# Decoder layer: in the feed-forward part each unit tile is projected four tiles later, ScalarE squares it twice and GpSimd subtracts

## Chip, cores and metric

The kernel runs on one core of one Trainium2 chip. The metric is device time in microseconds. A core has TensorE (PE in the profile, its weight loads PEld), VectorE (DVE), ScalarE (ACT), GpSimd (POOL) and the queue of SyncE (SP), each with its own instruction stream; they meet by semaphores only.

## What is computed

A decoder layer: linear attention, cross attention and a feed-forward part, each added to its input and normalised over the 256 features of a token. There are 8 batches of 512 tokens. The change touches the feed-forward part alone:

```python
def _L0_ffn_ref(x, fast_b, w_fc, w_proj, u, v, gate):
    ...
    h = _bitlinear(x, w_fc) + gate * (x @ v.T @ fast_b.T @ u.T)
    r = jnp.maximum(h, 0.0)
    return _bitlinear(r * r, w_proj)
...
x = _layernorm(x + _L0_ffn_ref(x, ...), axis=-1)
```

Here `h` has 1024 hidden units, and `_bitlinear` multiplies with a weight matrix that is rounded to three values and scaled.

## The kernel before

Features and hidden units lie on the 128 partitions, tokens in the free dimension. One batch of 512 tokens is 2 tiles of x (256 features) and 8 unit tiles (1024 hidden units), each 128 by 512. Every engine runs its own loop over the 8 batches, written out by hand in `ffn_phase`; the first two and the last two batches stand outside the loop, the four between them in a loop of two batches a turn. The order of the work on an engine is the order in its `batch` function, and nothing moves past a wait.

For precision a float is split in two: a rounded high part and the rest, the low part (`x_hi`, `x_lo`; `h_hi`, `h_lo`). The work on one unit tile i is:

- TensorE, `hidden`: six matmuls into one of the four PSUM banks `HIDDEN` (lines 47 to 49). It waits until ScalarE has read the bank's last content (`relu_out`).
- ScalarE, `hidden`: `r` = Relu of the bank (line 1294), and `h_hi` = Square of `r`, rounded (line 1298).
- GpSimd: `rr` = r * r, not rounded (line 1253).
- VectorE, `hidden_lo`: `h_lo` = `rr` - `h_hi` (line 1378).
- TensorE, `project`: for each of two output halves m, a matmul with `h_hi` and one with `h_lo` (lines 1478, 1479) into the accumulating bank `OUT[:, m]`. Half 0 of all eight tiles is done first, then half 1, after all eight `hidden` of the batch.

`r` and `rr` have four buffers each (RH = 4), so a tile may run four tiles ahead.

Around the unit tiles run two normalisations, of neighbouring batches. In the stretch that PE spends on batch b, the other work is:

- Norm 2 of batch b+1, which makes the input of the next batch: ScalarE squares (`norm2_square`, line 1268), VectorE adds two tiles (line 1334), TensorE `var2` (line 1453, a matmul in full float with a matrix of 1/256), ScalarE `norm2_root` (lines 1277, 1279, 1281), VectorE `normalise2` (lines 1354, 1357, 1365, 1370, 1372). Line 1372 writes `x_lo`, and the first `hidden` of batch b+1 waits for it.
- Norm 3 of batch b-1, the last step of that batch: VectorE `residual` (line 1385, two instructions, reads the banks `OUT`) and `sum_y3` (line 1334), TensorE `mean3` (line 1459), VectorE `deviate3` (line 1392) and `sum_squares3` (lines 1346, 1334), TensorE `var3` (line 1463), ScalarE `norm3_root`, VectorE `normalise3` (lines 1354, 1357, 1398), then the store on SP.

`norm3_root` is the last thing on ScalarE's list for a batch, and `normalise3` the last on VectorE's. The first projection of batch b overwrites `OUT` and waits for `residual(b-1)` (`y3_out`).

Of the kernel before, what the change touches and what calls it, by code (L numbers as in the profile page):

```python
# [16 lines left out]
ACT = mybir.ActivationFunctionType  # L17
ALU = mybir.AluOpType
# [6 lines left out]
P = 128  # L25
B, T, D = 8, 512, 256
DK = D // P
# [7 lines left out]
HK = HID // P  # L35
# [24 lines left out]
def f32(ap):  # L60
    return ap.bitcast(F32)
# [1116 lines left out]
def ffn_phase(nc, ctx, sb, a, c, ps, y2_dram, out):  # L1178
# [5 lines left out]
    tern = sb(ctx, "tern_r", [P, HK, D], F32R)  # L1184
    pscale = c["pscale"]

    def sems(*names):
# [11 lines left out]
    RH = 4  # L1199
    r = sb(ctx, "relu", [P, RH, T], F32)  # L1200
    rr = sb(ctx, "relu2", [P, RH, T], F32)
    h_hi, h_lo = (sb(ctx, "h_" + n, [P, HK, T], F32R) for n in ("hi", "lo"))
# [10 lines left out]
    x_split, h_ps, relu_out, hi_out, rr_out, lo_out, p_ps, y3_out = sems(  # L1213
        "x_split", "h_ps", "relu_out", "hi_out", "rr_out", "lo_out", "p_ps", "y3_out")
# [3 lines left out]
    OUT = ps[:, 5:7, :]  # L1218
# [4 lines left out]
    with nc.Block() as block:  # L1223
# [19 lines left out]
        @block.gpsimd  # L1243
        def _(pool):
            pool.tensor_copy(tern[:], c["tern"][:]).then_inc(tern_out, 1)

            def batch(b, first):
                for i in range(HK):
                    pool.wait_ge(relu_out, HK * b + i + 1)
                    if not (first and i < RH):  # L1250
                        pool.wait_ge(lo_out, HK * b + i - RH + 1)
                    n = i % RH
                    pool.tensor_tensor(rr[:, n, :], r[:, n, :], r[:, n, :], ALU.mult).then_inc(rr_out, 1)  # L1253

            batch(0, True)
            with pool.Fori(1, B) as b:
                batch(b, False)

        @block.scalar
        def _(act):  # L1260
            def norm2_square(b, par):
                if par:
                    act.wait_ge(y_in[1], 8 * (b - 1) + 16)
                elif not (isinstance(b, int) and b == 0):
                    act.wait_ge(y_in[0], 8 * b)
                if not (isinstance(b, int) and b == 0):
                    act.wait_ge(sq2_sum_out, b)
                act.activation(sq2[:], y2[:, par], ACT.Square).then_inc(sq2_out, 1)

            def norm_root(stat, norm, sems, b, first):  # L1270

                est, inv = norm
                var_ps, est_out, rs_out = sems
                act.wait_ge(var_ps, b + 1)
                if not first:
                    act.wait_ge(rs_out, 2 * b)
                act.activation(inv[:], stat, ACT.Ln, bias=c["eps"][:, 0:1]).then_inc(est_out, 1)  # L1277
                act.wait_ge(est_out, 3 * b + 1)
                act.activation(est[:], inv[:], ACT.Exp, scale=-0.5).then_inc(est_out, 1)
                act.wait_ge(est_out, 3 * b + 2)  # L1280
                act.activation(inv[:], est[:], ACT.Square).then_inc(est_out, 1)

            def norm2_root(b, first):
                norm_root(STAT2, (est2, inv2), (var2_ps, est2_out, rs2_out), b, first)

            def norm3_root(b, first):
                norm_root(STAT3, (est3, inv3), (var3_ps, est3_out, rs3_out), b, first)

            def hidden(b, i, first):
                n = HK * b + i  # L1290
                act.wait_ge(h_ps, n + 1)
                if not (first and i < RH):
                    act.wait_ge(rr_out, n - RH + 1)
                act.activation(r[:, i % RH, :], HIDDEN[i % RH], ACT.Relu).then_inc(relu_out, 1)  # L1294
                act.wait_ge(relu_out, n + 1)
                if i == 0 and not first:
                    act.wait_ge(p_ps, 2 * b)
                act.activation(h_hi[:, i, :], r[:, i % RH, :], ACT.Square).then_inc(hi_out, 1)

            def batch(b, par, first, second, last):  # L1300
                for i in (0, 1, 2):
                    hidden(b, i, first)
                if not last:
                    norm2_square(b + 1, 1 - par)
                for i in (3, 4):
                    hidden(b, i, first)
                for i in (5, 6, 7):
                    hidden(b, i, first)
                if not last:
                    norm2_root(b + 1, False)  # L1310
                if not first:
                    norm3_root(b - 1, second)

            act.preload_act_table_set("natural_log_exp_and_others")
            for k in range(DK):
                act.activation(w_hi[:, k], c["wfc"][:, k], ACT.Copy).then_inc(w_round, 1)
            norm2_square(0, 0)
            norm2_root(0, True)
            batch(0, 0, True, False, False)
            batch(1, 1, False, True, False)  # L1320
            with act.Fori(2, B - 3, 2) as i:
                batch(i, 0, False, False, False)
                batch(i + 1, 1, False, False, False)
            batch(B - 2, 0, False, False, False)
            batch(B - 1, 1, False, False, True)
            norm3_root(B - 1, False)

        @block.vector
        def _(dve):
# [41 lines left out]
                dve.wait_ge(x_split, 2 * b + 1)  # L1371
                dve.tensor_tensor(x_lo[:, par], x2[:, par], f32(x_hi[:, par]), ALU.subtract).then_inc(x_split, 1)  # L1372

            def hidden_lo(b, i):
                n = HK * b + i
                dve.wait_ge(hi_out, n + 1)
                dve.wait_ge(rr_out, n + 1)
                dve.tensor_tensor(h_lo[:, i, :], rr[:, i % RH, :], f32(h_hi[:, i, :]), ALU.subtract).then_inc(lo_out, 1)  # L1378

            def residual(b, par, first):  # L1380
                for m in range(DK):
                    dve.wait_ge(p_ps, 2 * b + m + 1)
# [20 lines left out]
            def batch(b, par, first, second, last):  # L1403
                if not first:
                    residual(b - 1, 1 - par, second)
                    sum_y3(b - 1, second)
                hidden_lo(b, 0)
                hidden_lo(b, 1)
                hidden_lo(b, 2)
                if not last:  # L1410
                    sum_squares2(b + 1, False)
                hidden_lo(b, 3)
                if not first:
                    deviate3(b - 1, second)
                for i in (4, 5):
                    hidden_lo(b, i)
                if not first:
                    sum_squares3(b - 1, second)
                for i in (6, 7):
                    hidden_lo(b, i)  # L1420
                if not last:
                    normalise2(b + 1, 1 - par, False)
                if not first:
                    normalise3(b - 1, second)
# [23 lines left out]
        def _(pe):  # L1448
# [16 lines left out]
            def hidden(b, par, i, first):  # L1465
                if i == 0:
                    pe.wait_ge(x_split, 2 * b + 2)
                if not (first and i < RH):
                    pe.wait_ge(relu_out, HK * b + i - RH + 1)
                cols = slice(i * P, (i + 1) * P)  # L1470
                split_matmul(pe, HIDDEN[i % RH], [(w_hi[:, k, cols], w_lo[:, k, cols], x_hi[:, par, k],
                                                   x_lo[:, par, k]) for k in range(DK)]).then_inc(h_ps, 1)

            def project(b, m, tiles):
                for k in tiles:
                    pe.wait_ge(lo_out, HK * b + k + 1)
                    w = tern[:, k, m * P:(m + 1) * P]
                    pe.matmul(OUT[:, m], w, h_hi[:, k, :], start=(k == 0), stop=False)
                    mm = pe.matmul(OUT[:, m], w, h_lo[:, k, :], start=False, stop=(k == HK - 1))
                if tiles[-1] == HK - 1:  # L1480
                    mm.then_inc(p_ps, 1)

            def batch(b, par, first, second, last):
                for i in (0, 1):
                    hidden(b, par, i, first)
                for i in (2, 3):
                    hidden(b, par, i, first)
                if not first:
                    mean3(b - 1, second)
                for i in (4, 5):  # L1490
                    hidden(b, par, i, first)
                if not last:
                    var2(b + 1, False)
                for i in (6, 7):
                    hidden(b, par, i, first)
                if not first:
                    pe.wait_ge(y3_out, 2 * b)
                project(b, 0, range(0, 6))
                if not first:
                    var3(b - 1)  # L1500
                project(b, 0, (6, 7))
                project(b, 1, range(HK))

            var2(0, True)
            pe.wait_ge(w_split, DK)
# [52 lines left out]
```

## Time and profile before

| | us |
|---|---|
| median of 3 runs | 1444.05 |
| lowest and highest | 1442.32, 1445.12 |
| the profiled execution's own time | 1441.72 |
| its span in the profile | 1439.9 |
| PE, DVE, ACT, POOL busy in the span | 1343.1, 956.8, 807.9, 621.9 |
| feed-forward part: first unit matmul to the end of the last instruction | 1238.64 to 1436.76 |

The feed-forward part is the last 198 us of the span. The busy shares of the whole span say little about it; it has to be read in its own window. An instruction's row gives its start, its duration, its engine, its line and, in brackets, for how long the engine had been idle and what ended that. On PE a matmul's record is longer than its share of the engine, since matmuls are pipelined: the distance from one start to the next is the cost.

### The profile page before, as it was taken

What the parts mean: (1) busy time and instruction counts of PE and PEld (TensorE: products, weight loads), DVE (VectorE), ACT (ScalarE), POOL (GpSimd) and SP (SyncE); (2) the same over time, 40 slices, a digit from 0 to 9 for tenths busy, and PEclk for the clock granted to TensorE, in tenths of its full rate; (3) what the DMA queues carried; (4) which work ended last, traced back from release to release, by engine and by line L of the source; (5) the groups of instructions that cost most, each with busy time, mean ns of one, the idle gap of its engine ahead of it and who ended that gap; (6) DMA issues with size and microseconds to landing.
All of it is one profiled execution on the core that took longest, in us unless ns stands there. A gap on an engine that the chain in (4) does not pass through costs nothing. (4 is left out here: it accounts for less than half of the span.)

```text
span 1439.9 us, 20724 instructions
## 1 busy us (share of the span) xinstructions
PE 1343.1 (93%) x7056; PEld 881.1 (61%) x7056; DVE 956.8 (66%) x1806; ACT 807.9 (56%) x1062; POOL 621.9 (43%) x312
## 2 busy tenths in 40 slices
PE   6999768999999999999999999999999997699995
PEld 4777545566566656656665665666566563466663
DVE  6678736765666576566667646666764664599996
ACT  2334435665656566565656656565665654565653
POOL 3513003553545355354535535453553543343432
PEclk9999979999999999999999999999999999799998
DMA  5211220000100100010010001001000100111101
GB/s 175 96 58 47 72 91 1 1 1 1 61 1 1 60 0 0 0 60 0 0 60 0 0 0 60 0 0 60 0 0 0 45 1 15 31 43 44 44 15 44
DMA packets 25535, 42.85 MB, mean 30 GB/s; under 512 B 3441, under 2 KB 7937, under 8 KB 25489
## 3 DMA queue, kind: packets, MB, share of 16 engines
q1 hardware_dynamic: 24672, 39.10, 8.0%
q0 software_dynamic: 816, 3.15, 0.6%
q8 instruction: 27, 0.44, 0.1%
q14 instruction: 20, 0.16, 0.0%
HBM read 29.66 MB, written 12.58 MB: 29 GB/s over the span
## 5 line engine op out<-in xcount | busy, mean ns | idle before, releaser
L907 DVE CUSTOM_DVE_ANT_0 junk<-ps,mask 128x512 bf16<-128x512 f32 x512 | 319.7, 686 | 98.0 <-PE ps L1039 96.8
L729 POOL TENSOR_TENSOR acc<-prob 128x1024 f32<-128x1024 f32 x64 | 153.2, 2394 | 489.1 <-ACT prob L773 489.1
L773 ACT ACTIVATE prob<-ps,mcol 128x1024 f32<-128x1024 f32 x256 | 282.2, 1117 | 135.3 <-PE ps L1033 128.7
L732 POOL TENSOR_TENSOR acc<-acc,prob 128x1024 f32<-128x1024 f32 x128 | 303.9, 2374 | 11.5
L1054 PE MATMUL ps<-prob,v_b 128*64 128x512 f32 x1024 | 244.5, 598 | 0.0
L1054 PEld LDWEIGHTS ps<-prob,v_b 128*64 128x64 f32 x1024 | 67.7, 136 | 133.0 <-issue 109.5
L912 DVE TENSOR_TENSOR ps<-ps,recip 128x512 f32<-128x512 f32 x64 | 44.8, 699 | 155.0 <-ACT recip L788 155.0
L1253 POOL TENSOR_TENSOR relu<-relu 128x512 f32<-128x512 f32 x64 | 79.9, 1252 | 109.1 <-ACT relu L1294 108.9
L1031 PE MATMUL ps<-q_hi,k_hi 64*128 64x512 f32 x512 | 114.7, 443 | 4.1 <-ACT prob L773 1.6
L1039 PE MATMUL ps<-k_hi,q_hi 64*128 64x512 f32 x512 | 103.0, 397 | 4.5 <-DVE nmx L907 2.0
L786 ACT ACTIVATE recip<-ps 128x512 f32<-128x512 f32 x64 | 38.2, 598 | 115.4 <-PE ps L1062 115.4
L1031 PE MATMUL ps<-q_hi,k_lo 64*128 64x512 f32 x512 | 101.6, 392 | 0.0
L1031 PE MATMUL ps<-q_lo,k_hi 64*128 64x512 f32 x512 | 101.6, 391 | 0.0
L1033 PE MATMUL ps<-shift,ones_r 64*128 64x512 f32 x512 | 101.3, 390 | 0.0
L1031 PEld LDWEIGHTS ps<-q_hi,k_hi 64*128 64x128 f32 x512 | 48.3, 184 | 54.7 <-ACT prob L773 24.3
L925 DVE SCALAR_TENSOR_TENSOR att_lo<-ps,bv,att_hi 128x512 fp32r<-128x512 f32 x64 | 48.0, 750 | 49.4 <-ACT att_hi L796 49.4
L1294 ACT ACTIVATE relu<-ps 128x512 f32<-128x512 f32 x64 | 38.2, 597 | 61.3 <-PE ps L49 58.1
L1378 DVE TENSOR_TENSOR h_lo<-relu,h_hi 128x512 fp32r<-128x512 f32 x64 | 62.9, 1021 | 10.7 <-POOL relu L1253 10.7
L796 ACT ACTIVATE att_hi<-ps,bv 128x512 fp32r<-128x512 f32 x64 | 44.1, 689 | 44.9 <-DVE ps L920 44.9
L1062 PE MATMUL ps<-acc,ones_w 128*64 128x512 f32 x256 | 65.8, 592 | 3.3 <-DVE att_lo L925 3.3
L816 ACT ACTIVATE v_b<-ps 128x512 f32<-128x512 f32 x64 | 38.4, 600 | 50.9 <-PE ps L49 50.9
L1045 PEld LDWEIGHTS ps<-ident,nmx 128*128 128x128 f32 x256 | 33.8, 192 | 53.4 <-issue 53.4
(205 smaller groups left out, 2917.0 us busy)
## 6 DMA issues: line engine op xcount, KB each, us to landing
x_in<-in_xT SPq DMA_DIRECT2D x8, 512.0 KB, 3.6
x_scratch<-x_a SPq DMA_DIRECT2D x8, 512.0 KB, 2.8
raw<-x_scratch SPq DMA_DIRECT2D x8, 512.0 KB, 5.1
raw<-in_cT SPq DMA_DIRECT2D x8, 512.0 KB, 6.0
x_res<-x_scratch SPq DMA_DIRECT2D x8, 512.0 KB, 4.5
y_scratch<-y SPq DMA_DIRECT2D x8, 512.0 KB, 3.1
y_c<-y_scratch SPq DMA_DIRECT2D x8, 512.0 KB, 3.6
outT<-x SPq DMA_DIRECT2D x8, 512.0 KB, 2.7
```

The lines of the kernel that those rows point to most:

```text
L729: pool.tensor_tensor(total, prob[:, 0], prob[:, 1], ALU.add).then_inc(acc_out, 1)
L732: pool.tensor_tensor(total, total, prob[:, kt], ALU.add).then_inc(acc_out, 1)
L773: act.activation(prob[:, i].rearrange("p h t -> p (h t)"), SCORE[i % 2].rearrange("p h t -> p (h t)"), ACT.Exp, scale=SCALE, bias=mcol[:, ...
L907: dve.tensor_tensor_reduce(junk[:, t % 2, h], SMAX[t % 2][:, h], mask[:], -1.0, -LOWEST, ALU.add, ALU.min, nmx[:, t, h * DH:h * DH + 1]).t ...
L925: dve.scalar_tensor_tensor(out=att_lo[:, p % HALF], in0=DEN, scalar=c["bv"][:, p:p + 1], in1=f32(att_hi[:, p % HALF]), op0=ALU.add, op1=AL ...
L1031: pe.matmul(banks[:, h], l[OWN[h], par, cols], r[OWN[h], par], start=(n == 0), stop=False)
L1033: mm = pe.matmul(banks[:, h], ones_r[OWN[h], :], shift[OWN[h], :], start=False, stop=True)
L1039: mm = pe.matmul(SMAX[t % 2][:, h], q_hi[OWN[h], par, toks], k_hi[OWN[h], par], start=True, stop=True)
L1054: mm = pe.matmul(PV[OWN[h], :], v[:, kt, cols], prob[:, kt, h, :], start=(kt == 0), stop=(kt == NT - 1))
L1062: mm = pe.matmul(DEN[OWN[h], :], c["ones_w"][:, 0:DH], acc[:, par, h, :], start=True, stop=True)
L1253: pool.tensor_tensor(rr[:, n, :], r[:, n, :], r[:, n, :], ALU.mult).then_inc(rr_out, 1)
L1378: dve.tensor_tensor(h_lo[:, i, :], rr[:, i % RH, :], f32(h_hi[:, i, :]), ALU.subtract).then_inc(lo_out, 1)
```

## The change

The work on a unit tile is dealt out anew, and the projection is woven into the units.

```diff
             def batch(b):
                 for i in range(HK):
-                    pool.wait_ge(relu_out, HK * b + i + 1)
-                    if not (first and i < RH):
-                        pool.wait_ge(lo_out, HK * b + i - RH + 1)
-                    n = i % RH
-                    pool.tensor_tensor(rr[:, n, :], r[:, n, :], r[:, n, :], ALU.mult).then_inc(rr_out, 1)
+                    pool.wait_ge(hi_out, HK * b + i + 1)
+                    pool.wait_ge(rr_out, HK * b + i + 1)
+                    pool.tensor_tensor(h_lo[:, i, :], rr[:, i % RH, :], f32(h_hi[:, i, :]),
+                                       ALU.subtract).then_inc(lo_out, 1)
...
                 act.activation(h_hi[:, i, :], r[:, i % RH, :], ACT.Square).then_inc(hi_out, 1)
+                if not (first and i < RH):
+                    act.wait_ge(lo_out, n - RH + 1)
+                act.activation(rr[:, i % RH, :], r[:, i % RH, :], ACT.Square).then_inc(rr_out, 1)
 
             def batch(b, par, first, second, last):
-                for i in (0, 1, 2):
+                for i in (0, 1):
                     hidden(b, i, first)
                 if not last:
                     norm2_square(b + 1, 1 - par)
-                for i in (3, 4):
-                    hidden(b, i, first)
-                for i in (5, 6, 7):
+                for i in (2, 3, 4, 5):
                     hidden(b, i, first)
                 if not last:
                     norm2_root(b + 1, False)
+                for i in (6, 7):
+                    hidden(b, i, first)
                 if not first:
                     norm3_root(b - 1, second)
...
-            def project(b, m, tiles):
+            def project(b, tiles):
                 for k in tiles:
                     pe.wait_ge(lo_out, HK * b + k + 1)
-                    w = tern[:, k, m * P:(m + 1) * P]
-                    pe.matmul(OUT[:, m], w, h_hi[:, k, :], start=(k == 0), stop=False)
-                    mm = pe.matmul(OUT[:, m], w, h_lo[:, k, :], start=False, stop=(k == HK - 1))
-                if tiles[-1] == HK - 1:
-                    mm.then_inc(p_ps, 1)
+                    for m in range(DK):
+                        w = tern[:, k, m * P:(m + 1) * P]
+                        pe.matmul(OUT[:, m], w, h_hi[:, k, :], start=(k == 0), stop=False)
+                        mm = pe.matmul(OUT[:, m], w, h_lo[:, k, :], start=False, stop=(k == HK - 1))
+                        if k == HK - 1:
+                            mm.then_inc(p_ps, 1)
...
-                for i in (0, 1):
+                for i in (0, 1, 2, 3):
                     hidden(b, par, i, first)
-                for i in (2, 3):
-                    hidden(b, par, i, first)
                 if not first:
                     mean3(b - 1, second)
-                for i in (4, 5):
-                    hidden(b, par, i, first)
+                    pe.wait_ge(y3_out, 2 * b)
+                project(b, (0,))
+                hidden(b, par, 4, first)
+                project(b, (1,))
                 if not last:
                     var2(b + 1, False)
-                for i in (6, 7):
+                for i in (5, 6, 7):
                     hidden(b, par, i, first)
-                if not first:
-                    pe.wait_ge(y3_out, 2 * b)
-                project(b, 0, range(0, 6))
+                    project(b, (i - 3,))
+                project(b, (5, 6))
                 if not first:
                     var3(b - 1)
-                project(b, 0, (6, 7))
-                project(b, 1, range(HK))
+                project(b, (7,))
```

`hidden_lo` and its eight calls a batch are gone from VectorE; what is left there keeps its order. ScalarE's Relu loses its wait on `rr_out`.

Two places of the order matter below. The first is TensorE's list at the end of a batch. Before, `var3` (mean_w times sq_sum, waiting for `c_sq3_sum_out`) stood after six tiles of half 0:

```order
L1478 MATMUL ps<-h_hi,tern_r 128x512 [waits c_lo_out]
L1479 MATMUL ps<-h_lo,tern_r 128x512
L1463 MATMUL ps<-sq_sum,mean_w 128x512 [waits c_sq3_sum_out]
L1476 REGISTER_ALU
L1478 MATMUL ps<-h_hi,tern_r 128x512 [waits c_lo_out]
L1479 MATMUL ps<-h_lo,tern_r 128x512
```

After it came ten tiles of projection (20 matmuls) and then the next batch. In the changed kernel it stands behind tile 6, with the four matmuls of tile 7 between it and the next batch's first unit:

```order
L1464 MATMUL ps<-h_hi,tern_r 128x512 [waits c_lo_out]
L1465 MATMUL ps<-h_lo,tern_r 128x512
L1464 MATMUL ps<-h_hi,tern_r 128x512
L1465 MATMUL ps<-h_lo,tern_r 128x512
L1448 MATMUL ps<-sq_sum,mean_w 128x512 [waits c_sq3_sum_out]
L1461 REGISTER_ALU
L1464 MATMUL ps<-h_hi,tern_r 128x512 [waits c_lo_out]
L1465 MATMUL ps<-h_lo,tern_r 128x512
L1464 MATMUL ps<-h_hi,tern_r 128x512
L1465 MATMUL ps<-h_lo,tern_r 128x512
L1452 REGISTER_ALU
L1454 ISA [waits c_x_split]
```

So 16 of the 20 matmuls that stood between `var3` and the next batch are now ahead of `var3`.

The second place is ScalarE's list around `norm2_root` of the next batch (the three rows of `est2`). Before, it came after tile 7, and `norm3_root` (`var3_ps`) followed at once:

```order
L1294 ACTIVATE relu<-ps 128x512 [waits c_rr_out,c_h_ps]
L1298 ACTIVATE h_hi<-relu 128x512 [waits c_relu_out]
L1274 REGISTER_ALU
L1276 REGISTER_ALU [waits c_var2_ps]
L1277 ACTIVATE inv<-ps,eps 128x512 [waits c_rs2_out]
L1278 ISA
L1279 ACTIVATE est<-inv 128x512 [waits c_est2_out]
L1280 REGISTER_ALU
L1281 ACTIVATE inv<-est 128x512 [waits c_est2_out]
L1276 ISA [waits c_var3_ps]
```

Now two whole unit tiles, of three instructions each, stand behind it:

```order
L1275 ACTIVATE inv<-ps,eps 128x512 [waits c_rs2_out]
L1276 ISA
L1277 ACTIVATE est<-inv 128x512 [waits c_est2_out]
L1278 REGISTER_ALU
L1279 ACTIVATE inv<-est 128x512 [waits c_est2_out]
L1289 REGISTER_ALU
L1290 ACTIVATE relu<-ps 128x512 [waits c_h_ps]
L1294 ACTIVATE h_hi<-relu 128x512 [waits c_relu_out]
L1297 ACTIVATE relu<-relu 128x512 [waits c_lo_out]
```

The root for the next batch moved ahead of the last two tiles, and line 1297 is the second Square (the rows call both `r` and `rr` "relu").

## Rows read from the trace of the kernel before

**Rows 1.** Windows: length, busy PE, PEld, DVE, ACT, POOL, clock, DMA, GB/s.

```profile
1330.00:1354.00 24.00, 21.90 (x87) 15.96 (x88) 23.44 (x24) 14.48 (x23) 9.80 (x8) 1.00 0.14 45
1427.00:1440.00 13.00, 2.08 (x2) 0.50 (x2) 5.42 (x6) 1.95 (x3) 0.00 (x0) 0.50 0.11 40
```

**Rows 2.** Groups by line in the feed-forward part, VectorE's subtraction.

```profile
L1378 DVE TENSOR_TENSOR h_lo<-relu,h_hi 128x512 fp32r<-128x512 f32 x64 | 62.9, 1021 | 10.7 <-POOL relu L1253 10.7
```

**Rows 3.** Timeline: the first unit matmul of batches 0, 2, 4 and 7.

```profile
1238.64 0.76 PE L47 MATMUL ps<-cx_hi,wfc_hi 128*128 128x512 f32 x1 [6.95 <-DVE cx_lo L1372]
1282.57 0.49 PE L47 MATMUL ps<-cx_hi,wfc_hi 128*128 128x512 f32 x1 [0.21 <-DVE cx_lo L1372]
1330.08 0.49 PE L47 MATMUL ps<-cx_hi,wfc_hi 128*128 128x512 f32 x1 [0.40 <-DVE cx_lo L1372]
1401.08 0.50 PE L47 MATMUL ps<-cx_hi,wfc_hi 128*128 128x512 f32 x1
```

**Rows 4.** Timeline of batch 4: GpSimd and VectorE at the same time.

```profile
1332.60 1.40 DVE L1385 SCALAR_TENSOR_TENSOR y<-ps,pscale,x 128x512 f32<-128x512 f32 x2
1333.98 1.04 POOL L1253 TENSOR_TENSOR relu<-relu 128x512 f32<-128x512 f32 x1 [0.33 <-ACT relu L1294]
1334.04 1.52 DVE L1334 TENSOR_TENSOR y_sum<-y 128x512 f32<-128x512 f32 x1
...
1344.21 2.06 DVE L1346 TENSOR_TENSOR sq<-dev 128x1024 f32<-128x1024 f32 x1
1345.24 1.93 POOL L1253 TENSOR_TENSOR relu<-relu 128x512 f32<-128x512 f32 x1
```

**Rows 5.** Timeline of batch 4 on TensorE, the last unit matmul before mean3, and behind it.

```profile
1335.44 0.39 PE L49 MATMUL ps<-cx_hi,wfc_lo 128*128 128x512 f32 x1
1335.70 1.12 PE L1459 MATMUL ps<-y_sum,mean_w 128*128 128x512 f32 x2
1336.89 0.39 PE L48 MATMUL ps<-cx_lo,wfc_hi 128*128 128x512 f32 x1
```

**Rows 6.** GpSimd's subtraction early in the kernel (line 241); VectorE's cast (timeline).

```profile
L241 POOL TENSOR_TENSOR wq_lo<-raw,wq_hi x4: 1265/1272/2135, 23.7 to 30.9; 128x512 fp32r<-128x512 f32 x4
53.52 1.67 DVE L426 CAST og_hi<-sq_a 128x1024 fp32r<-128x1024 f32 x1
```

**Rows 7.** Timeline of ScalarE: two roots' ends, and three unit instructions in a row.

```profile
1231.73 0.69 ACT L1277 ACTIVATE inv<-ps,eps 128x512 f32<-128x512 f32 x1 [2.89 <-PE ps L1453]
1233.11 0.63 ACT L1281 ACTIVATE inv<-est 128x512 f32<-128x512 f32 x1
...
1248.14 0.58 ACT L1294 ACTIVATE relu<-ps 128x512 f32<-128x512 f32 x1
1248.75 0.63 ACT L1298 ACTIVATE h_hi<-relu 128x512 fp32r<-128x512 f32 x1
1249.29 0.58 ACT L1294 ACTIVATE relu<-ps 128x512 f32<-128x512 f32 x1
```

**Rows 8.** Timeline of VectorE: the steps of the normalisation.

```profile
1233.77 0.75 DVE L1354 SCALAR_TENSOR_TENSOR rs<-ps,eps,inv 128x512 f32<-128x512 f32 x1 [3.07 <-ACT inv L1281]
1325.82 0.69 DVE L1357 SCALAR_TENSOR_TENSOR rs<-rs,est 128x512 f32<-128x512 f32 x1
1326.64 1.22 DVE L1365 SCALAR_TENSOR_TENSOR x<-y_c,rs 128x1024 f32<-128x1024 f32 x1
1327.99 0.69 DVE L1370 CAST cx_hi<-x 128x1024 fp32r<-128x1024 f32 x1
1328.72 1.23 DVE L1372 TENSOR_TENSOR cx_lo<-x,cx_hi 128x1024 fp32r<-128x1024 f32 x1
```

**Rows 9.** Timeline of the tail: last projection, mean3, var3.

```profile
1422.70 0.39 PE L1479 MATMUL ps<-h_lo,tern_r 128*128 128x512 f32 x1
1425.45 1.12 PE L1459 MATMUL ps<-y_sum,mean_w 128*128 128x512 f32 x2 [2.36 <-DVE y_sum L1334]
1429.88 2.08 PE L1463 MATMUL ps<-sq_sum,mean_w 128*128 128x512 f32 x2 [3.30 <-DVE sq_sum L1334]
```

More of the change, by code:

```diff
@@ L1245, in _, with batch @@
             pool.tensor_copy(tern[:], c["tern"][:]).then_inc(tern_out, 1)
-            def batch(b, first):
+            def batch(b):
                 for i in range(HK):
-                    pool.wait_ge(relu_out, HK * b + i + 1)
-                    if not (first and i < RH):
-                        pool.wait_ge(lo_out, HK * b + i - RH + 1)
-                    n = i % RH
-                    pool.tensor_tensor(rr[:, n, :], r[:, n, :], r[:, n, :], ALU.mult).then_inc(rr_out, 1)
-            batch(0, True)
-            with pool.Fori(1, B) as b:
-                batch(b, False)
+                    pool.wait_ge(hi_out, HK * b + i + 1)
+                    pool.wait_ge(rr_out, HK * b + i + 1)
+                    pool.tensor_tensor(h_lo[:, i, :], rr[:, i % RH, :], f32(h_hi[:, i, :]),
+                                       ALU.subtract).then_inc(lo_out, 1)
+            with pool.Fori(0, B) as b:
+                batch(b)
         @block.scalar
@@ L1291, in hidden @@
                 act.wait_ge(h_ps, n + 1)
-                if not (first and i < RH):
-                    act.wait_ge(rr_out, n - RH + 1)
                 act.activation(r[:, i % RH, :], HIDDEN[i % RH], ACT.Relu).then_inc(relu_out, 1)
@@ L1372, in normalise2 @@
                 dve.tensor_tensor(x_lo[:, par], x2[:, par], f32(x_hi[:, par]), ALU.subtract).then_inc(x_split, 1)
[L1374 to L1378, printed above, removed]
             def residual(b, par, first):
@@ L1406, in batch @@
                     sum_y3(b - 1, second)
-                hidden_lo(b, 0)
-                hidden_lo(b, 1)
-                hidden_lo(b, 2)
                 if not last:
                     sum_squares2(b + 1, False)
-                hidden_lo(b, 3)
                 if not first:
                     deviate3(b - 1, second)
-                for i in (4, 5):
-                    hidden_lo(b, i)
                 if not first:
                     sum_squares3(b - 1, second)
-                for i in (6, 7):
-                    hidden_lo(b, i)
                 if not last:
@@ L1489, in batch @@
                     mean3(b - 1, second)
-                for i in (4, 5):
-                    hidden(b, par, i, first)
+                    pe.wait_ge(y3_out, 2 * b)
+                project(b, (0,))
+                hidden(b, par, 4, first)
+                project(b, (1,))
                 if not last:
                     var2(b + 1, False)
-                for i in (6, 7):
+                for i in (5, 6, 7):
                     hidden(b, par, i, first)
-                if not first:
-                    pe.wait_ge(y3_out, 2 * b)
-                project(b, 0, range(0, 6))
+                    project(b, (i - 3,))
+                project(b, (5, 6))
                 if not first:
                     var3(b - 1)
-                project(b, 0, (6, 7))
-                project(b, 1, range(HK))
+                project(b, (7,))
             var2(0, True)
```

## The prediction

> **What bounds the kernel now.** I read the feed-forward part alone, by three views. The timeline gives the first unit matmul of each batch [rows 3]: batches 0 and 1 take 43.93 us together (21.97 each), batches 2 to 6 take 118.50 (23.70 each), and from batch 7's first matmul to the end, at 1436.76, it is 35.68. The sum is 198.1. The windows show who is full [rows 1]: in 24 us of a steady batch VectorE is busy 23.44, TensorE 21.90 (its records overlap), ScalarE 14.48, GpSimd 9.80. So VectorE sets the batch. The groups say with what [rows 2]: 64 subtractions, 62.9 us, 7.9 us a batch, 1021 ns each.
>
> Why 1021 ns, for an instruction that takes 0.68 alone? Rows 4 show it. GpSimd works from 1333.98 to 1335.02. VectorE's y_sum, begun at 1334.04, ends at 1335.56, 0.54 after GpSimd. The square of 1024 columns ends at 1346.27, and GpSimd's product, begun under it at 1345.24, ends 0.90 behind that. So these two never run together: the later one ends a full duration less 0.15 after the earlier. The two residual instructions, which read PSUM, run beside a product of GpSimd at their usual 0.7. I call instructions with two SBUF inputs on VectorE "exclusive"; the cast behaves like one too (1.67 at 53.52 against 0.69 alone) [rows 6, 8].
>
> The Trainium skill agrees, in "GPSIMD Engine Reference", Key points: GpSimd shares its SBUF interfaces with VectorE and contends with instructions of two SBUF inputs or in a two-port mode.
>
> **Unit costs.** TensorE, start to start: from 1330.08 to 1335.44 are 23 matmuls, 0.1 of it start-up, so 0.229 each [rows 3, 5]. A unit tile is 6 x 0.229 = 1.37, a projected tile 4 x 0.229 = 0.91. A full-float matmul: from 1335.44 to 1336.89 with two ordinary ones in it, 1.45 - 0.46 = 0.98 [rows 5]. TensorE's own work in a batch is 8 x 1.37 + 8 x 0.91 + 3 x 0.98 = 21.2.
>
> ScalarE: Relu to Square is 0.61, Square to an independent instruction 0.54 [rows 7]. The second Square is not in the trace; its nearest row is the first, 0.63. So a tile is now 0.61 + 0.54 + 0.54 = 1.7, against 1.15, and a root is 1231.73 to 1233.74, 2.0 [rows 7]. ScalarE's sum, 8 x 1.7 + 2 x 2.0 + 1.0 = 18.6, fits beside 21.2.
>
> GpSimd: the subtraction from two tiles to a rounded one is line 241: 1.27 at its least [rows 6], against 1.04 for r * r [rows 4]. Bounds: 1.04 below, 2.13 above (the stretched maximum there). I take 1.27, since shapes and types are the same. Eight are 10.2 us; with VectorE's exclusive ones (about 9.0) that is 19.2, under 21.2.
>
> The Trainium skill, in "GPSIMD Engine Reference", Engine selection, speaks against the move: elementwise work with two inputs is about 2 times slower on GpSimd than on VectorE. By it the subtraction would be some 1.35 (twice 0.68) instead of 1.27, an estimate, and the sum below about 1.3 us higher. That GpSimd is the slower one agrees with the rows (1.27 against 0.68).
>
> So by busy time alone the batch would fall from 23.7 to about 21.2. The question is whether the waits allow it.
>
> **The ring.** I lay one batch out with these costs; 0 is its first unit matmul.
>
> 1. The norm 3 root of the batch before ends at 1.37 on ScalarE (its place follows from step 6). VectorE then needs 0.77 + 0.82 + 1.16 for the three steps of normalise3, 1.4 for the two residuals [rows 4, 8], and is at y_sum at 5.6. There GpSimd has just begun tile 1 (5.40 to 6.67), so y_sum ends at 6.67 + 0.54 = 7.2.
> 2. TensorE has done tiles 0 to 3 at 5.5 and stands at mean3 until 7.34: a wait of 1.85. Behind it in the queue are all the rest.
> 3. mean3 0.98, projection of tile 0 0.91, unit 4 1.37, projection 1 0.91, var2 0.98, unit 5 1.37: 13.85. ScalarE starts tile 5 at 14.13, is through at 15.84, and the root for the next batch ends at 17.85.
> 4. VectorE: two steps (0.77, 0.82), then x from 19.47 to 20.70, exclusive [rows 8]. ScalarE meanwhile does tile 6 and hands it over at 19.71. GpSimd has to wait for x: 20.70 + 1.27 - 0.15 = 21.82.
> 5. TensorE, ready for tile 6 since 20.2, gets it at 21.93: a wait of 1.7. Then 0.91 and 0.1 start-up, var3 at 22.94, 0.98, and tile 7 at 23.91 (its subtraction is done at 23.5, behind the cast). 0.91 more: the next batch starts at 24.82. x_lo, held up by both, ends at 24.56, just in time.
> 6. var3's result is there at 24.06, the root runs from 24.18 to 26.19, which is 1.37 in the next batch. The ring is closed.
>
> **A steady batch is 24.8 us, 1.1 more than before.** What carried it: before, 20 matmuls stood behind var3 and hid the root and normalise3 (about 4.6 us of cover). Now there are four; so the chain root, normalise3, residual, y_sum, mean3 lies bare, and in the same lap TensorE waits for x, which comes late because mean3 came late. The 7.9 us that VectorE loses are not on this ring, apart from the h_lo instructions that it no longer meets.
>
> **The sum.** Batch 0 has no norm 3 and starts at the low clock as before; the same laying-out gives 23.4 (21.92 before), since its end has the collision of step 4 too. Batch 1, with mean3 in time, gives 23.1 (22.01 before). Batches 2 to 6: 5 x 24.82 = 124.1, against 118.5. Batch 7: TensorE ends at 22.0, but norm 3 of batch 6 runs only behind var3, so y_sum is done at 28.3 and mean3 starts at 28.45, against 24.37 in the rows (1425.45 - 1401.08) [rows 3, 9]. From there it is the same chain. That is 4.1 more. TensorE has then stood idle for over 6 us; in the rows it ran var3 at half clock after a pause of 3.3, in 2.08 instead of 1.12 [rows 1, 9], so mean3 costs 0.96 more as well.
>
> 1.5 + 1.1 + 5.6 + 4.1 + 0.96 gives 13.3. Before's own time of 1441.7 becomes 1455.0. The median of the runs shown is 2.3 above that execution; on its scale it is 1457.3. I say 1457.
>
> **Rivals.**
>
> - *The exclusion does not bite (12 in 100).* If the new subtraction ran beside VectorE, steps 1, 4 and 5 lose their stretches: y_sum ends at 6.3, tile 6 is there at 21.0 at once. The same laying-out then gives 23.05 a batch. 198.1 becomes about 199.5: time 1445, no difference that can be told. Against it: rows 4, where every meeting shows it; for it: the rows are of a product of one tile with itself.
> - *GpSimd comes first at tile 6 (8 in 100).* In step 4 x is 0.24 ahead. If GpSimd wins, tile 6 is 1.1 earlier and the lap is about 24.0: time 1452.
> - *TensorE becomes the bound: faster (8 in 100).* If the chain behind var3 and the one behind var2 were both covered, the batch would be TensorE's 21.2: 7 x (21.2 - 23.2) is 14 less, the tail's 4 to 5 come on top, time 1434. It decides from the point where the lap without stretches, 23.05, is 1.8 shorter than I lay out; no row is that far off.
> - *The subtraction is slow, near 2.1 (4 in 100).* GpSimd and VectorE together then exceed 25 a batch: 7 x 2 us more, time above 1465. For it: only the one stretched row [rows 6].
> - The ring as laid out: 68 in 100, with a range of its own of 1451 to 1462 (subtraction 1.04: 3 less; 1.5: 4 more).
>
> **The numbers.** Predicted 1457. From 1445 (no exclusion) to 1463 about 8 in 10 are covered. A measurement tells 0.2%, some 3 us, from no change: slower 0.80, same 0.12, faster 0.08.
>
> **What the profile of the changed kernel should show.** VectorE's busy time in a steady 24 us falls from 23.4 to about 15 to 16, ScalarE's rises to about 19; neither is full. Starts of batches 24.8 apart. TensorE idle before mean3 (line 1444), waiting for y_sum, about 1.8 us, and before line 1464 at tile 6, waiting for h_lo, about 1.7, in each of batches 2 to 6. GpSimd's subtraction alone 1.27, stretched to 2.1 at tile 6; VectorE's cast and x_lo stretched to 1.5 and 2.2. mean3 of the last batch 28 us after its first matmul and at half clock. I am wrong if the waits at mean3 are missing, or if the batches stand under 23.5 apart.

## The result

| | before | changed |
|---|---|---|
| median, us | 1444.31 (1442.32 to 1445.12, 4 runs) | 1453.09 (1451.56 to 1457.09, 4 runs) |
| ratio to before | | 1.007 (95% interval 1.0057 to 1.0084) |
| own time of the profiled execution | 1441.72 | 1457.09 |
| feed-forward part in the trace | 198.1 | 208.7 |

The changed kernel is 0.7% slower. Its profiled execution entered the feed-forward part 4.7 us later than that of before (1243.37 against 1238.64 [rows 3]), though nothing ahead of it was changed, so the two own times should not be compared. The granted clock was at half for 59.5 us ahead of that point, against 47.3 us in the execution of before; whether that is all of the 4.7 is not shown. The feed-forward parts can be compared, and differ by 10.6 us. The interval of the ratio is 8 to 12 us.

The page of the changed kernel, with each engine's busy time in the whole span:

```profile
PE 1347.8 (93%) x7056; PEld 885.8 (61%) x7056; DVE 907.4 (62%) x1742; ACT 837.8 (58%) x1126; POOL 636.9 (44%) x312
```

And the window of one steady batch, 24 us long, columns as in [rows 1]:

```profile
1338.96:1362.96 24.00, 21.02 (x85) 15.73 (x85) 16.54 (x15) 17.63 (x31) 11.90 (x8) 1.00 0.13 44
```

VectorE fell from 23.44 to 16.54, ScalarE rose to 17.63, GpSimd to 11.90. No engine is full any more (TensorE is busy for 21.02 of the 24 us), and yet the batch is longer. Something waits. The view of waits in the feed-forward part says for what (engine, line, releaser, us in total, times, longest; other waits left out at the dots):

```profile
...
DVE rs L1353 <- ACT inv L1279: 63.8, 16, 11.3
...
ACT inv L1275 <- PE ps L1448: 30.9, 8, 12.4
PEld ps L1464 <- POOL h_lo L1251: 16.7, 15, 1.8
PE ps L1444 <- DVE y_sum L1333: 15.1, 7, 6.0
...
PE ps L1464 <- POOL h_lo L1251: 10.0, 8, 1.4
...
DVE dev L1385 <- PE ps L1444: 6.6, 7, 2.2
```

TensorE now waits at mean3 (line 1444) for y_sum and at a projection (line 1464) for GpSimd's subtraction; VectorE waits for both roots, and ScalarE for var3 (line 1448). The timeline of TensorE over the end of batch 4, 1338.96 being that batch's start, shows both waits and the next start:

```profile
1346.27 1.12 PE L1444 MATMUL ps<-y_sum,mean_w 128*128 128x512 f32 x2 [1.59 <-DVE y_sum L1333]
...
1360.59 0.50 PE L1464 MATMUL ps<-h_hi,tern_r 128*128 128x512 f32 x1 [1.39 <-POOL h_lo L1251]
...
1361.64 1.02 PE L1448 MATMUL ps<-sq_sum,mean_w 128*128 128x512 f32 x2
...
1363.44 0.49 PE L47 MATMUL ps<-cx_hi,wfc_hi 128*128 128x512 f32 x1
```

The bracket counts from the modelled end of the last matmul. By starts, less the 0.229 us of one matmul, TensorE stood idle 1.75 us before mean3 (1344.29 to 1346.27) and 1.55 us before the projection of tile 6 (1358.81 to 1360.59). The batch took 24.48 us. The chain of the work that ended last, in that stretch, goes round once (start, us, what; "issue" is time with no wait that the profile shows):

```profile
1339.58 0.64 ACT inv L1279
1340.25 0.76 DVE rs L1353
1341.03 0.70 DVE rs L1356
...
1342.99 1.42 DVE y L1378 x2
1344.43 1.72 DVE y_sum L1333
...
1346.27 1.12 PE ps L1444 x2
...
1352.87 0.61 ACT relu L1290
...
1358.37 2.17 POOL h_lo L1251
1360.59 0.50 PE ps L1464
...
1361.80 0.87 PE ps L1448 x2
1362.78 0.70 ACT inv L1275
```

It leaves ScalarE's root of norm 3, passes VectorE, mean3, unit tile 5, ScalarE's root of norm 2 and its work on tile 6, GpSimd's subtraction of tile 6 and var3, and is back at the same root, whose first step began at 1338.19 in the lap before and begins at 1362.78 in this one, 24.6 us later.

The instructions stretched by the exclusion, on VectorE and on GpSimd in the same batch (alone they take 0.69, 1.23 and 1.29):

```profile
1359.54 1.54 DVE L1369 CAST cx_hi<-x 128x1024 fp32r<-128x1024 f32 x1
1361.12 2.19 DVE L1371 TENSOR_TENSOR cx_lo<-x,cx_hi 128x1024 fp32r<-128x1024 f32 x1
1358.37 2.17 POOL L1251 TENSOR_TENSOR h_lo<-relu,h_hi 128x512 fp32r<-128x512 f32 x1 [2.28 <-ACT relu L1297]
1360.50 1.73 POOL L1251 TENSOR_TENSOR h_lo<-relu,h_hi 128x512 fp32r<-128x512 f32 x1
```

And the tail, where mean3 of the last batch, after a pause of 6 us, ran at the lower of the clock's two levels (granted clock 0.50 from 1439.85 to 1441.95; 2.07 us instead of 1.12 in [rows 9]):

```profile
1439.85 2.07 PE L1444 MATMUL ps<-y_sum,mean_w 128*128 128x512 f32 x2 [5.99 <-DVE y_sum L1333]
```

### The profile page after: what moved, and what is told of

It is laid out like the page before. It is cut to its first block and busy times, and to the rows that moved or that the text cites. A ratio compares the mean times of both kernels' runs of the same rounds, so it can differ in the third digit from the quotient of the medians.

```text
span 1455.3 us, 20590 instructions
## 1 busy us (share of the span) xinstructions
PE 1347.8 (93%) x7056; PEld 885.8 (61%) x7056; DVE 907.4 (62%) x1742; ACT 837.8 (58%) x1126; POOL 636.9 (44%) x312
## 5 line engine op out<-in xcount | busy, mean ns | idle before, releaser
L1251 POOL TENSOR_TENSOR h_lo<-relu,h_hi 128x512 fp32r<-128x512 f32 x64 | 94.4, 1482 | 107.0 <-ACT relu L1297 106.9
L47 PE MATMUL ps<-bc_hi,wk_hi 128*128 128x512 f32 x128 | 54.0, 422 | 11.7 <-DVE bc_lo L881 11.7
L1464 PE MATMUL ps<-h_hi,tern_r 128*128 128x512 f32 x128 | 55.1, 431 | 10.0 <-POOL h_lo L1251 10.0
```

What stands on the lines that cost most here:

```text
L47: pe.matmul(out, lh, rh, start=(i == 0), stop=False)
L1251: pool.tensor_tensor(h_lo[:, i, :], rr[:, i % RH, :], f32(h_hi[:, i, :]), ALU.subtract).then_inc(lo_out, 1)
```

## The experiments

All eight were timed in rounds with the kernel before on the same chip; its median there was 1443.17 beside e1 to e4 and 1442.54 beside e5 to e8. For each the table gives the median, the ratio to before, and from its trace a steady batch (mean of batches 2 to 6), the tail (batch 7's first matmul to the end) and the whole feed-forward part, in us. For the two kernels of the study, a steady batch is 23.70 and 24.39, the tail 35.7 and 40.1, the part 198.1 and 208.7.

| run | median | ratio (95%) | batch | tail | part |
|---|---|---|---|---|---|
| e1 changed, var3 early | 1440.14 | 0.9978 (0.9967 to 0.999) | 22.74 | 35.7 | 195.6 |
| e2 division of work alone | 1440.97 | 0.9986 (0.9975 to 0.9998) | 23.04 | 33.9 | 197.0 |
| e3 order alone | 1463.69 | 1.0144 (1.0127 to 1.0161) | 24.93 | 40.1 | 217.7 |
| e4 changed, rs in PSUM | 1446.82 | 1.0027 (1.0017 to 1.0037) | 23.53 | 40.1 | 201.9 |
| e5 e1, root of norm 2 early | 1433.28 | 0.9936 (0.992 to 0.9953) | 21.69 | 35.7 | 188.9 |
| e6 e5, square of norm 2 first | 1428.02 | 0.9898 (0.9882 to 0.9915) | 20.88 | 36.4 | 184.1 |
| e7 e6, rs in PSUM | 1429.42 | 0.991 (0.989 to 0.9929) | 20.87 | 36.5 | 183.4 |
| e8 before, var3 late | 1450.78 | 1.0057 (1.004 to 1.0073) | 23.97 | 42.3 | 206.7 |

### e1: var3 early

```diff
-                for i in (5, 6, 7):
+                for i in (5, 6):
                     hidden(b, par, i, first)
                     project(b, (i - 3,))
-                project(b, (5, 6))
+                hidden(b, par, 7, first)
                 if not first:
                     var3(b - 1)
-                project(b, (7,))
+                project(b, (4, 5, 6, 7))
```

> Changed kernel with one edit: on TensorE the variance matmul of norm 3 (var3) stands right behind unit tile 7 instead of behind the projection of tile 6, so 16 matmuls of projection and not 4 lie between it and the next batch. Theory (the ring through var3, root, normalise3, residual, y_sum, mean3): the wait at mean3, 1.5 us in each steady batch of the changed kernel's trace, is gone, and with it the delay that it passes on; a steady batch falls from 24.4 to about 23.0 us, the last batch's tail from 40.1 to about 36.5, the feed-forward part from 208.7 to about 198, the time to about 1442. Rival (the exclusion of GpSimd and VectorE at tile 6 sets the batch, and would set it anyway): the wait at mean3 goes but comes back at tile 6; the batch stays within 0.3 of 24.4, and only the tail gains 3 us: about 1449.

Measured: 1440.14, batch 22.74, tail 35.7. The theory's numbers hold (1442, about 23.0, about 36.5 were expected), and the rival (24.4 within 0.3) falls. The waits of TensorE in that run's steady batch, by its timeline:

```profile
1337.12 1.12 PE L1444 MATMUL ps<-y_sum,mean_w 128*128 128x512 f32 x2
...
1348.07 1.02 PE L1448 MATMUL ps<-sq_sum,mean_w 128*128 128x512 f32 x2
1351.45 0.50 PE L1464 MATMUL ps<-h_hi,tern_r 128*128 128x512 f32 x1 [0.52 <-POOL h_lo L1251]
1353.14 0.50 PE L1464 MATMUL ps<-h_hi,tern_r 128*128 128x512 f32 x1 [0.48 <-POOL h_lo L1251]
```

mean3 starts without a bracket: it waits for nobody. One matmul, moved ahead of twelve projection matmuls (2.7 us), takes all of the loss back and a little more. What is left are two short waits for the subtractions of tiles 6 and 7.

### e2: the division of work alone

The changed kernel with TensorE's `project` and `batch` and ScalarE's `batch` of the kernel before; ScalarE squares twice and GpSimd subtracts.

> One part of the change alone: ScalarE squares twice and GpSimd subtracts, but TensorE and ScalarE keep the order of the kernel before (half 0 of all tiles, then half 1, var3 with ten tiles of projection behind it, both roots behind tile 7). Theory (order, not the division of work, costs the time): var3's chain is covered again; about 23.4 us a steady batch, tail as in the kernel before or 1 us shorter, time 1440 to 1445. Rival (the slower subtraction on GpSimd, 1.29 against 0.68, costs the time): 24.4 us a batch as in the changed kernel, about 1450 or more.

Measured: 1440.97, batch 23.04. The theory holds and the rival falls: with the old order the slower subtraction does not make the kernel slower (it leaves one short wait, 0.43 in the second row below), and taking eight subtractions from VectorE gains 0.7 us a batch. That is little beside the 7.9 us of VectorE's time that they were, because the batch now ends at another wait:

```profile
1335.84 0.49 PE L47 MATMUL ps<-cx_hi,wfc_hi 128*128 128x512 f32 x1 [1.12 <-DVE cx_lo L1371]
1353.49 0.50 PE L1463 MATMUL ps<-h_hi,tern_r 128*128 128x512 f32 x1 [0.43 <-POOL h_lo L1251]
1358.98 0.49 PE L47 MATMUL ps<-cx_hi,wfc_hi 128*128 128x512 f32 x1 [1.12 <-DVE cx_lo L1371]
```

The two batches shown begin 1.12 us late for x_lo: ScalarE starts the root of norm 2 at 1351.92, directly behind tile 7's second Square (1351.40 to 1352.01), and VectorE's x_lo ends at 1358.86.

### e3: the order alone

The kernel before with the changed TensorE and ScalarE orders; GpSimd multiplies and VectorE subtracts.

> The other part alone: TensorE's and ScalarE's new order, but GpSimd multiplies and VectorE subtracts as in the kernel before. Theory: the chain behind var3 lies bare here too, with VectorE's eight subtractions on top of it; laid out from the rows of the kernel before it is 24.8 us a steady batch, tail 38 to 39: about 1455 to 1460. Rival (the division of work costs it, the order is harmless): 23.7 us a batch as before, 1444.

Measured: 1463.69, batch 24.93, tail 40.1, batches 0 and 1 25.8 and 27.2. The harm is in the order, and is larger with the old division of work: 20.5 us against the 8.8 of both parts together. The rival (1444) falls. The batch of 24.93 is close to the 24.8 that I expected, but the mechanism that I gave for it is not what the trace shows: in the steady batches TensorE does not wait at mean3 at all (its one wait there, 6.0 us, is in the tail). It waits at the start of every next batch for x_lo. The waits of the whole part, and then of four batches (1316 to 1416):

```profile
PE ps L1459 <- DVE y_sum L1334: 6.0, 1, 6.0
```

```profile
PE ps L47 <- DVE cx_lo L1372: 10.0, 4, 2.5
```

The end of batch 3 shows where x_lo is held up:

```profile
1334.24 2.04 DVE L1378 TENSOR_TENSOR h_lo<-relu,h_hi 128x512 fp32r<-128x512 f32 x2 [1.00 <-POOL relu L1253]
1336.21 0.74 DVE L1354 SCALAR_TENSOR_TENSOR rs<-ps,eps,inv 128x512 f32<-128x512 f32 x1
...
1339.89 1.23 DVE L1372 TENSOR_TENSOR cx_lo<-x,cx_hi 128x1024 fp32r<-128x1024 f32 x1
1341.25 0.49 PE L47 MATMUL ps<-cx_hi,wfc_hi 128*128 128x512 f32 x1 [2.53 <-DVE cx_lo L1372]
```

Here `normalise2` stands behind `hidden_lo` of tile 7 on VectorE's list, and the woven order brings tile 7 later (its Relu begins 16.9 us into the batch). In the changed kernel VectorE has no `hidden_lo`, so this wait is not in it, and this run does not test the ring of the changed kernel; e1 does. That the forecast of the batch came out was luck.

The time lies 4 us above the range that I gave, and the two batches that stick out are 1 and 4, with 27.2 and 26.1. In both the granted clock was at half for a stretch (columns as in [rows 1]):

```profile
1263.90:1270.70 6.80, 6.13 (x14) 4.79 (x15) 3.32 (x5) 1.82 (x3) 1.04 (x1) 0.50 0.20 70
1342.40:1345.80 3.40, 3.40 (x10) 2.62 (x9) 3.24 (x5) 1.23 (x2) 1.04 (x1) 0.50 0.30 112
```

At half clock a matmul takes 0.43 us from start to start instead of 0.229. Batch 4 is 1.4 us longer than its neighbours. For batch 1 about 3 us is an estimate, from half of the 6.1 us of it at half clock. So part of the 20.5 us is the clock's, which the changed kernel lost only at its start and in its tail.

### e4: the reciprocal roots in PSUM

```diff
-                inverse_root((STAT2, est2, inv2, rs2), est2_out, rs2_out, b)
+                inverse_root((STAT2, est2, inv2, STAT2), est2_out, rs2_out, b)
...
-                dve.scalar_tensor_tensor(out=x2[:, par], in0=y2[:, par], scalar=-0.5, in1=both(rs2), op0=ALU.mult,
+                dve.scalar_tensor_tensor(out=x2[:, par], in0=y2[:, par], scalar=-0.5, in1=both(STAT2), op0=ALU.mult,
```

The same for norm 3; `var2` and `mean3` then wait for `x2_out` and `x3_out` instead of `rs2_out` and `rs3_out`.

> Changed kernel, but the reciprocal roots rs of both norms are written in place into their PSUM banks, so that the second step of each root and the products x and x3 have one SBUF input and one PSUM input and should run beside GpSimd. Theory (exclusion): GpSimd's subtraction of tile 6 takes 1.29 and not 2.17, TensorE's wait at tile 6 falls by 0.9, a steady batch from 24.4 to about 23.6, the first two by 0.9 each; the wait at mean3 stays near 1.5: feed-forward part 208.7 to about 203, time about 1447. Rival (the stretch comes from something else, such as the two instructions' memory traffic in general): tile 6's subtraction stays above 2 us and the time at 1453.

Measured: 1446.82, batch 23.53, part 201.9: as the theory said. Its timeline of VectorE and GpSimd at tile 6:

```profile
1352.38 1.22 DVE L1364 SCALAR_TENSOR_TENSOR x<-y_c,ps 128x1024 f32<-128x1024 f32 x1
1352.54 1.29 POOL L1251 TENSOR_TENSOR h_lo<-relu,h_hi 128x512 fp32r<-128x512 f32 x1 [2.28 <-ACT relu L1297]
1353.73 0.69 DVE L1369 CAST cx_hi<-x 128x1024 fp32r<-128x1024 f32 x1
```

x (1352.38 to 1353.60) and the subtraction (1352.54 to 1353.83) overlap by 1.06 us and neither is stretched; in the changed kernel the same pair gave 1.23 and 2.17. What the edit changed in this pair is that one of x's inputs comes from PSUM. The step that now writes rs into PSUM takes what it took before, 0.70 against 0.69 us. What the edit takes of the exclusion was worth 6.3 us by the medians (1453.09 to 1446.82) and 6.8 by the traces (208.7 to 201.9).

### e5: the root of norm 2 early, on top of e1

```diff
-                for i in (2, 3, 4, 5):
+                for i in (2, 3):
                     hidden(b, i, first)
                 if not last:
                     norm2_root(b + 1, False)
-                for i in (6, 7):
+                for i in (4, 5, 6, 7):
                     hidden(b, i, first)
...
                 project(b, (0,))
+                if not last:
+                    var2(b + 1, False)
                 hidden(b, par, 4, first)
                 project(b, (1,))
-                if not last:
-                    var2(b + 1, False)
```

> On top of the early var3: the root of norm 2 for the next batch stands two unit tiles earlier on ScalarE (behind tile 3, not 5) and its variance matmul right behind the projection of tile 0. Theory (with mean3 on time, the next thing that ends last in a batch is normalise2 colliding with the subtractions of tiles 6 and 7): moved away from them, a steady batch falls from 22.8 us to about 21.8, batch 0 by 0.5: feed-forward part about 189, time 1433. Rival (TensorE's own work, 21.2 by its rows, plus small gaps is already the bound at 22.8): no change, 1440.

Measured: 1433.28, batch 21.69, part 188.9: the theory to the microsecond; the rival falls.

### e6: the square of norm 2 first, on top of e5

```diff
-                for i in (0, 1):
-                    hidden(b, i, first)
                 if not last:
                     norm2_square(b + 1, 1 - par)
-                for i in (2, 3):
+                for i in (0, 1, 2, 3):
                     hidden(b, i, first)
```

> On top of that, the square for norm 2 stands first in ScalarE's batch instead of behind tile 1, where it can run while TensorE makes the first unit tile. Theory: the variance matmul no longer comes late, normalise2 is through before tile 6, and the batch is TensorE's own work, about 21.1 to 21.4 us; feed-forward part 184 to 186, time about 1429. Rival (ScalarE is the bound by then): 21.8 as in the run before it.

Measured: 1428.02, 1.0% under the kernel before; the part of 184.1 is as expected, and the batch of 20.88 lies a little under the 21.1 to 21.4 that I gave. The rival (21.8) falls. The window of a steady stretch, columns as in [rows 1]:

```profile
1339.00:1363.00 24.00, 24.00 (x99) 18.31 (x98) 21.07 (x18) 20.73 (x37) 15.51 (x10) 1.00 0.13 44
```

TensorE is busy for all of the 24 us and at full clock: the feed-forward part is bound by TensorE's own work, 20.88 a batch. This version beats both kernels, and no other is measurably faster.

### e7: rs in PSUM, on top of e6

> The kernel of the run before with rs of both norms kept in PSUM. Theory: once TensorE is the bound, the exclusion of GpSimd and VectorE costs nothing, so the 6.3 us that this edit gave the changed kernel are no longer there: within 1 us of the run before. Rival (the stretches still delay TensorE): 3 to 6 us less than the run before.

Measured: 1429.42, that is 1.4 us above e6 where I expected at most 1; single runs lie between 1426.9 and 1432.29, and the intervals of e6 and e7 overlap. The rival (3 to 6 us less) falls. The steady batch is the same (20.87); only batch 0 is 0.7 us shorter. The edit that was worth 6.3 us in the changed kernel is worth nothing measurable here. In e6 instructions are still stretched (in this batch x 2.12, the cast 1.58, a subtraction 2.03), but TensorE, busy all the time in the window above, does not wait for any of them:

```profile
1336.91 2.12 DVE L1362 SCALAR_TENSOR_TENSOR x<-y_c,rs 128x1024 f32<-128x1024 f32 x1
1339.16 1.58 DVE L1367 CAST cx_hi<-x 128x1024 fp32r<-128x1024 f32 x1
1338.15 2.03 POOL L1251 TENSOR_TENSOR h_lo<-relu,h_hi 128x512 fp32r<-128x512 f32 x1 [0.21 <-ACT relu L1297]
```

### e8: the kernel before with var3 late

```diff
-                project(b, 0, range(0, 6))
+                project(b, 0, range(HK))
+                project(b, 1, range(0, 6))
                 if not first:
                     var3(b - 1)
-                project(b, 0, (6, 7))
-                project(b, 1, range(HK))
+                project(b, 1, (6, 7))
```

> The kernel before with one edit: var3 stands in front of the last four projection matmuls (tiles 6 and 7 of half 1) instead of in front of the last twenty. Theory (what hides the root and normalise3 is the projection behind var3, whoever subtracts): a steady batch rises from 23.7 to 24.2 or more, and the tail from 35.7 by 4 to 6 us with its mean3 at half clock: feed-forward part 198 to about 207, time 1450 to 1455. Rival (the place of var3 matters only with the new division of work): 1443 in the batches, at most 4 us in the tail.

Measured: 1450.78, 8.2 us more than before for one moved matmul, of about the size of the whole change. The time is in the range, but not put together as I expected: the tail took most of it (42.3 against 35.7, 6.6 us where I gave 4 to 6), and a steady batch rose by 0.27 alone, less than 0.5. In the steady batches the result is thus nearer to the rival than to the theory, though the wait at mean3 is there:

```profile
1338.59 1.12 PE L1459 MATMUL ps<-y_sum,mean_w 128*128 128x512 f32 x2 [1.72 <-DVE y_sum L1334]
```

In the kernel before, VectorE's work was the limit (busy for 23.23 of the 23.78 us of batch 3), and TensorE had slack beside it. By starts, TensorE stood idle there for 1.3 us at var2, 0.7 at var3 and 0.6 for x_lo, 2.6 together; in e8 it is 1.9 at mean3 and 0.9 for a subtraction, 2.7 together. The new wait took the place of the old ones.

## Why the prediction was right

The forecast was 1457 in a range of 1445 to 1463, slower with 0.8; measured were 1453.09. The likeliest case was the one that came.

- **The ring (steps 1 to 6).** Right for the changed kernel, and shown by e1: with var3 moved and nothing else, the wait at mean3 is gone, and the batch falls from 24.39 to 22.74. The laps' pieces, as laid out and as in the trace of batch 4: root's end to mean3's start 5.97 and 6.06; mean3 to tile 5's Relu 6.79 and 6.60; that to x's start 5.34 and 5.32; x to the projection of tile 6 2.46 and 2.40; that to the next start 2.89 and 2.85; start to root's end 1.37 and 1.25. The sum is 24.82 and 24.48. The largest miss is the full-float matmul, sized 0.98 from a row that held some start-up of TensorE as well. Between running neighbours it takes 0.86, from the start of var2 to the second matmul behind it, 1.09, less one ordinary matmul, 0.229:

```profile
1350.43 1.02 PE L1438 MATMUL ps<-sq_sum,mean_w 128*128 128x512 f32 x2
1350.89 0.79 PE L47 MATMUL ps<-cx_hi,wfc_hi 128*128 128x512 f32 x1
1351.52 0.39 PE L48 MATMUL ps<-cx_lo,wfc_hi 128*128 128x512 f32 x1
```

  With it TensorE's own work is 20.8 a batch and not 21.2, which fits the 20.88 of e6.
- **The exclusion.** Right: tile 6's subtraction 2.17 (2.1 forecast), the cast 1.54, x_lo 2.19 (1.5 and 2.2). e4 shows the cause, and the price of the part that it takes away.
- **The subtraction's price.** 1.29 alone, against 1.27 from [rows 6]; so the rival of a subtraction near 2.1 fell. e2 shows that this price was not what cost the time. The Trainium skill's factor of 2 over VectorE ("GPSIMD Engine Reference", Engine selection) fits as well (1.29 over 0.68 is 1.9).
- **The rival of GpSimd first at tile 6** did not come: x began first in all seven batches, in batch 4 by 0.18 us (1358.19 against 1358.37; 0.24 forecast). That is a narrow margin.
- **The rival of no exclusion** was at 1445; the measured time lies beyond it, and e4 shows that the exclusion is real. Its 23.05 a batch was not tested: e4 takes away the part of x and x3 and has a batch of 23.53, with y_sum still stretched (1.56 to 1.74 us in the steady batches, against 0.69 alone) and mean3 still waiting.
- **The rival of TensorE as the bound** was right on what stands in the way (the chains behind var3 and var2) and it is what e5 and e6 reach by covering both.
- **The sum, 13.3**, was too large. Against the 10.6 of the traces: batches 2 to 6 gave 3.5 and not 5.6, that is 0.4 a batch less; batch 1 gave 0.6 and not 1.1; the tail 4.4 and not 5.1; and batch 0 gave 2.2 and not 1.5, since TensorE ran at half clock for its first 5.4 us and not 3.9 as in the kernel before, and half of that difference, an estimate of what the clock cost, is the missing 0.7. The term that was mis-sized is the steady batch, for the reason above. The clock's 0.7 has nothing to do with the change and hid part of that miss by chance. The median says 8.8; the rest, 1.8, lies within its interval.
- **The busy times** that I named were a little off: VectorE 16.5 (15 to 16), ScalarE 17.6 (about 19). Nothing hung on them.

## What to carry to other kernels

Taking a third of the work off the fullest engine gives nothing if the same edit moves the producer of a long cross-engine chain to the end of a queue: count what stands in the queue behind the instruction that starts such a chain, for that is its cover (20 matmuls before, 4 after). Lay one lap out from the rows and see whether it comes out longer than the own work of the fullest engine; if so, the waits on it tell which single instruction to move. Where another engine's work is the limit, a short cover costs little in the steady batches (0.27 us each in e8) and shows in the tail. The same new order can close another ring when the work is dealt out differently (e3), so an experiment with half of a change need not test the mechanism of the whole. Once no engine is full, stretches from two engines that exclude each other cost time only where the ring passes through them: 6.3 us in one order, nothing measurable in another.

## What the runs showed of the hardware

- When a VectorE instruction with two SBUF inputs, or VectorE's cast, meets a GpSimd one, they run one after the other, whichever began first: x 1.23 and the subtraction behind it 2.17; y_sum, begun at 1344.43 under a subtraction, 1.71 instead of 0.69. With one of the two inputs in PSUM they overlap and neither is stretched. That is e4, and the changed kernel itself has such a pair, VectorE's deviation with the mean in PSUM:

```profile
1346.93 1.29 POOL L1251 TENSOR_TENSOR h_lo<-relu,h_hi 128x512 fp32r<-128x512 f32 x1 [1.33 <-ACT relu L1297]
1347.43 1.22 DVE L1385 TENSOR_TENSOR dev<-y,ps 128x1024 f32<-128x1024 f32 x1 [0.69 <-PE ps L1444]
```

  The kernel before had it at the residual (1332.60 to 1334.00 in [rows 4]), beside this product:

```profile
1332.60 1.04 POOL L1253 TENSOR_TENSOR relu<-relu 128x512 f32<-128x512 f32 x1 [9.23 <-ACT relu L1294]
```

  New to me was that a result and an input can be moved to PSUM on purpose to escape the exclusion, at no cost to VectorE's instruction (1.22).
- TensorE's clock did not follow the length of a pause alone. In the last batch mean3 came after a wait of 4.03 us at full clock in e1 and after 4.04 us at half clock in e6:

```profile
1423.88 1.13 PE L1444 MATMUL ps<-y_sum,mean_w 128*128 128x512 f32 x2 [4.03 <-DVE y_sum L1333]
```

```profile
1411.11 2.07 PE L1442 MATMUL ps<-y_sum,mean_w 128*128 128x512 f32 x2 [4.04 <-DVE y_sum L1331]
```

In e1 the granted clock was 1.00 up to 1424.90, the first 1.0 us of mean3, and 0.50 behind it; in e6 it had fallen to 0.50 at 1411.07, just before mean3. What decides between them was not tried.
